# A linear-attention and quantised-ffn layer on one core: another order of the DMA queue, and another first turn

## The reference

```
xn  = LN(x)
q,k = elu(xn @ Wq.T + bq) + 1,  elu(xn @ Wk.T + bk) + 1      # 16 heads of 32 features
v   = xn @ Wv.T + bv
num = sum over d of q[t,d] * cumsum_t(k[t,d] * v[t,e])       # causal linear attention
den = max(sum over d of q[t,d] * cumsum_t(k[t,d]), 1e-6)
att = (num / den) @ Wo.T + bo
y   = x + LN(att)
yq  = y quantised in blocks of 32 features to the nearest value of an fp6 grid, times its block scale
wd  = the ffn weight, quantised in the same way
out = y + LN(yq @ wd.T + bias)
```

## Time and profile before

| | |
|---|---|
| median of the runs | 2397.83 us |
| the profiled execution | 2399.21 us, span 2397.4 us, mean granted clock 0.993 |
| TensorE matmuls | 2332.0 us busy, 97% |
| VectorE | 1984.1 us, 83% |
| GpSimd | 1470.3 us, 61% |
| ScalarE | 1080.8 us, 45% |
| DMA | 195.55 MB, 82 GB/s, 24.5% of 16 engines |

### The profile page before, as it was taken

One profiled execution on the slowest core, in us unless ns is written; L12 is line 12 of the kernel. 1 busy time (PEld: TensorE's weight loads), 2 busy tenths in 40 slices (PEclk: granted clock), 3 DMA queues, 4 the chain that ended last, 5 costly groups with the idle time before them and its releaser, 6 DMA issues.

```text
span 2397.4 us, 63827 instructions
## 1 busy us (share of the span) xinstructions
PE 2332.0 (97%) x26146; PEld 1905.0 (79%) x26146; DVE 1984.1 (83%) x3988; ACT 1080.8 (45%) x1840; POOL 1470.3 (61%) x1730
## 2 busy tenths in 40 slices
PE   7999999999999999999999999999999999999997
PEld 5877888888788788888787887888878888878785
DVE  7888889888788888898888887888988888878886
ACT  4444444444444444444444444444444444444442
POOL 2566566666566665666665665656666656656554
PEclk9999999999999999999999999999999999999999
DMA  4222221222222322222322222222123222223211
GB/s 158 71 92 98 75 77 62 88 99 73 86 65 75 99 90 80 77 65 86 99 73 90 73 71 91 96 76 75 62 89 99 73 90 73 71 91 95 77 46 37
DMA packets 108227, 195.55 MB, mean 82 GB/s; under 512 B 15136, under 2 KB 21664, under 8 KB 107424
## 3 DMA queue, kind: packets, MB, share of 16 engines
q1 hardware_dynamic: 107936, 191.47, 24.5%
HBM read 155.65 MB, written 35.78 MB: 80 GB/s over the span
## 4 chain that ended last, share of the span: by engine, by line
PE 79%; DMA 7%; DVE 4%; ACT 3%; issue 3%; POOL 2%; SPq 2%; POOLq 0%; DVEq 0%; ACTq 0%
PE work L423 12%; PE work L425 11%; PE work L424 11%; PE score L423 10%; PE score L424 10%; PE score L425 10%; PE work L540 5%; PE work L442 4%; PE score L505 4%; DMA rden_dram<-rinv 3%; DMA kc<-rden_dram 3%; PE state_bank L553 1%; POOL f_buf L1425 1%; DVE A L1020 1%; PE score L527 1%
## 5 line engine op out<-in xcount | busy, mean ns | idle before, releaser
L1020 DVE TENSOR_TENSOR A<-score,causal 128x512 f32<-128x512 f32 x512 | 329.2, 681 | 21.5 <-PE score L505 21.5
L1395 POOL TENSOR_TENSOR exp_t<-exp_t,x_coef 128x512 f32<-128x512 f32 x124 | 198.5, 1601 | 148.6 <-DMA exp_t<-in_xt 148.6
L725 ACT CAST oT_hi<-kc 128x512 fp32r<-128x512 f32 x128 | 79.6, 622 | 365.4 <-DVE kc L1015 365.4
L1402 POOL TENSOR_TENSOR x_res<-x_res,o_buf 128x512 f32<-128x512 f32 x128 | 175.6, 1372 | 104.5 <-ACT o_buf L670 104.5
L423 PE MATMUL work<-wo_hi,oT_hi 128*128 128x512 f32 x512 | 204.2, 399 | 14.8 <-ACT Kn L720 11.9
L423 PE MATMUL work<-wv_hi,xT_hi 128*128 128x512 f32 x512 | 214.9, 420 | 0.0
L423 PE MATMUL score<-xT_hi,wq_hi 128*128 128x512 f32 x512 | 208.1, 406 | 6.8 <-DVE KT L960 6.8
L1397 POOL TENSOR_TENSOR exp_t<-exp_t,x_coef 128x512 f32<-128x512 f32 x124 | 205.2, 1655 | 9.7
L423 PE MATMUL score<-xT_hi,wk_hi 128*128 128x512 f32 x512 | 205.7, 402 | 0.0
L425 PE MATMUL work<-wv_hi,xT_lo 128*128 128x512 f32 x512 | 202.2, 395 | 0.6 <-issue 0.6
L424 PE MATMUL work<-wv_lo,xT_hi 128*128 128x512 f32 x512 | 201.8, 394 | 0.9 <-issue 0.9
(11 more groups left out here) (134 smaller groups left out, 6393.1 us busy)
## 6 DMA issues: line engine op xcount, KB each, us to landing
x_in<-in_x SPq DMA_DIRECT2D x128, 256.0 KB, 4.3
x_res<-in_x SPq DMA_DIRECT2D x128, 256.0 KB, 2.8
kc<-rden_dram SPq DMA_DIRECT2D x128, 256.0 KB
exp_t<-in_xt SPq DMA_DIRECT2D x124, 256.0 KB, 3.1
out<-f_buf SPq DMA_DIRECT2D x96, 256.0 KB, 2.0
x_coef<-coef_dram SPq DMA_DIRECT2D x31, 512.0 KB, 3.8
out<-xd SPq DMA_DIRECT2D x32, 256.0 KB, 2.1
rden_dram<-rinv SPq DMA_DIRECT2D x32, 64.0 KB, 3.5
```

The costliest lines, as they stand in the source:

```text
L1020: nc.vector.tensor_tensor(A[:, j, :, :], score_bank[j][:], causal[:].unsqueeze(1).to_broadcast([P, G, P]), ALU.mult).then_inc(a_set, 1)
L1395: nc.gpsimd.tensor_tensor(rows, rows, by_token(0), ALU.mult).then_inc(x_scaled, 1)
L1402: nc.gpsimd.tensor_tensor(x_res[:, b, :], x_res[:, b, :], o_buf[:, b % 2, :], ALU.add).then_inc(r_set, 1)
```

## The change

- SyncE's order in a turn is rewritten. x by rows is loaded two tiles ahead (load_x(i + 2, b)), spread over the turn; the store and the spreads of the reciprocals go ahead of the loads of x by features, which are interleaved with the spreads; load_res(1), (2) and (3) go to the end of the turn, behind the last store and load_x(i + 2, 3).
- Wo is staged in x_res instead of kc, is loaded last of the weights, and is split behind the Q products; load_res of tile 0 waits for that. Wv comes before it.
- The last step of quantising the ffn weight, the product of the fp8 values with the scales, is made by GpSimd (dequantise_wf), no longer by VectorE.
- wf_transposes(0) and (1) run behind q(3), (2) and (3) behind v(0), through the banks work[2], work[1], work[2], work[0].
- The lists of ScalarE, VectorE and GpSimd are reordered to go with it, in the first turn and in the others.

```diff
-        W_DONE = {"k": G, "q": G + 1, "o": G + 2, "v": G + 3}
+        W_DONE = {"k": G, "q": G + 1, "v": G + 2, "o": G + 3}
-        wf_bank = [work[0], work[1]]
+        wf_bank = [work[2], work[1], work[2], work[0]]
...
             def load_res(tile, b):
                 if tile > 0:
                     sp.wait_ge(out_set, count(tile - 1, b))
+                else:
+                    sp.wait_ge(w_lo_set, W_DONE["o"])
...
             def turn(i, prev, cur, nxt):       # SyncE, as it is after
+                after = i + 2 < TILES
                 store(i - 1, 0)
                 load_x(i + 2, 0)
                 load_x(i + 2, 1)
                 store_coef(i + 1)
                 spread_coef(i + 1)
                 store(i - 1, 1)
                 load_x(i + 2, 2)
                 store_rden(i)
                 spread_rden(i, 0)
                 load_xt(i + 1, 0)
                 spread_rden(i, 1)
                 load_xt(i + 1, 1)
                 store(i - 1, 2)
                 spread_rden(i, 2)
                 load_res(i, 0)
                 load_xt(i + 1, 2)
                 spread_rden(i, 3)
                 load_xt(i + 1, 3)
                 store(i - 1, 3)
                 load_x(i + 2, 3)
                 load_res(i, 1)
                 load_res(i, 2)
                 load_res(i, 3)
...
+            for b in range(NSEQ):              # ahead of turn 0
+                load_x(1, b)
```

TensorE, first turn:

```diff
+                q(2)
+                q(3)
                 if first:
                     wf_transposes(0)
                     wf_transposes(1)
-                q(2)
-                q(3)
-                if first:
-                    wf_transposes(2)
-                    wf_transposes(3)
                 f(2)
                 xd_transposes(3)
                 past_products()
                 denominators()
                 v(0)
+                if first:
+                    wf_transposes(2)
+                    wf_transposes(3)
                 scores(0)
                 kn(0)
```

The end of the lists in the other turns, where the prediction looks:

```diff
 VectorE                                    # around normalise(0)
                 f_bias(3)
                 normalise(0)
-                o_lo(0)
-                f_seen(3)
                 mask(1, 0)
+                f_seen(3)
                 mask(1, 1)
+                o_lo(0)
+                x_lo(i + 1, 0)
                 v_bias(1)
...
                 greatest(i, 0)
                 scale(i, 0)
-                x_lo(i + 1, 3)
+                x_lo(i + 1, 2)
                 quantise(i, 0)
+                x_lo(i + 1, 3)
+                o_bias(i, 2)
                 normalise(3)
-                o_bias(i, 2)
-                r_seen(i, 1)
+                o_seen(i, 2)
                 o_lo(3)
+                r_seen(i, 1)
                 join(i, "r", 1)
                 widen(i, "r", 1)
 ScalarE
-                seed(0)
                 kn(0)
+                seed(0)
+                kn(1)
                 o_hi(0)
-                seed(1)
                 x_hi(i + 1, 0)
                 f_norm(2)
-                kn(1)
+                seed(1)
+                seed(2)
                 x_hi(i + 1, 1)
                 o_hi(1)
                 o_norm(i, 0)
 GpSimd
                 rstd(i - 1, "f", 1)
                 output(1)
+                rstd(i - 1, "f", 2)
                 x_scale(i + 1, 0)
-                rstd(i - 1, "f", 2)
+                output(2)
                 x_scale(i + 1, 1)
-                output(2)
                 rstd(i - 1, "f", 3)
```

More of the change, by code:

```diff
@@ L354, in turn @@
             def turn(i, prev, cur, nxt):
[L355 to L359, removed]
+                after = i + 2 < TILES
                 if prev:
                     store(i - 1, 0)
-                if cur:
-                    load_res(i, 0)
+                if after:
+                    load_x(i + 2, 0)
+                    load_x(i + 2, 1)
                 if nxt:
@@ L368, in turn @@
                     store(i - 1, 1)
[L369 to L373, removed]
+                if after:
+                    load_x(i + 2, 2)
                 if cur:
@@ L388, in turn @@
                     store(i - 1, 3)
+                if after:
+                    load_x(i + 2, 3)
                 if cur:
+                    load_res(i, 1)
+                    load_res(i, 2)
                     load_res(i, 3)
@@ L479, in v @@
                         take(pe, i, ("v", b), here, before)
+                        if first and b == 0:
+                            pe.wait_ge(wf_lo_set, 2)
                         weights(i, "v")
@@ L512, in kn @@
                         take(pe, i, ("kn", b), here, before)
+                        if first and b == 0:
+                            pe.wait_ge(wf_lo_set, G)
                         transposes(bank(("kn", b)), lambda g: KT[:, g, b, SEG - P:SEG]).then_inc(kn_tr, 1)
@@ L734, in seed @@
                     if cur:
+                        if first and b == 0:
+                            act.wait_ge(wf_lo_set, 3)
                         take(act, i, ("att", b), {0} if first else {-1, 0}, set())
@@ L767, in turn @@
                     k(2)
-                    carry(0)
-                    wf_high(0)
-                    wf_high(1)
                     k(3)
-                    carry(1)
                     q(0)
                     q(1)
+                    carry(0)
+                    q(2)
+                    carry(1)
                     carry(2)
-                    q(2)
+                    wf_high(0)
                     q(3)
+                    wf_high(1)
+                    high("o")
                     carry(3)
+                    for j in range(HPG):
+                        past(j)
                     wf_high(2)
                     wf_high(3)
-                    for j in range(HPG):
-                        past(j)
                     kn(0)
                     seed(0)
+                    o_hi(0)
                     seed(1)
-                    o_hi(0)
                     kn(1)
@@ L824, in turn @@
                 k(2)
+                o_norm(i - 1, 3)
                 carry(0)
-                o_norm(i - 1, 3)
+                k(3)
+                carry(1)
+                r_norm(i - 1, 2)
                 xd_hi(1)
-                r_norm(i - 1, 2)
-                carry(1)
                 r_norm(i - 1, 3)
-                k(3)
-                q(0)
-                carry(2)
-                f_norm(0)
+                f_norm(0)
+                carry(2)
+                q(0)
                 xd_hi(2)
@@ L856, in turn @@
                 kn(2)
-                seed(2)
+                o_hi(2)
+                seed(3)
+                kn(3)
                 f_norm(3)
@@ L1236, in turn @@
                 join(i - 1, "o", 3)
-                scan(0)
+                r_seen(i - 1, 2)
                 widen(i - 1, "o", 3)
                 phi_k(1)
-                r_seen(i - 1, 2)
+                scan(0)
+                phi_k(2)
                 scan(1)
                 f_bias(0)
-                phi_k(2)
-                if nxt:
-                    widen(i + 1, "x", 1)
                 join(i - 1, "r", 2)
+                f_seen(0)
                 widen(i - 1, "r", 2)
                 r_seen(i - 1, 3)
-                if nxt:
-                    x_seen(i + 1, 3)
@@ L1277, in turn @@
                     widen(i + 1, "x", 3)
+                phi_q(0)
+                phi_q(1)
+                xd_lo(2)
+                phi_q(2)
+                product(2)
+                phi_q(3)
+                f_seen(1)
                 join(i - 1, "f", 1)
-                phi_q(3)
-                product(2)
                 widen(i - 1, "f", 1)
                 product(3)
-                f_bias(2)
                 xd_lo(3)
-                f_seen(2)
                 clamp()
                 invert()
-                join(i - 1, "f", 2)
+                f_bias(2)
@@ L1478, in turn @@
                 dequantise(i - 1, 2)
+                output(0)
                 if nxt:
                     rstd(i + 1, "x", 2)
-                output(0)
+                product(0)
                 dequantise(i - 1, 3)
-                product(0)
                 product(1)
```

202 lines of the change are left out of this document (102 added, 100 removed).

## The result

The changed kernel takes 2459.43 us, median of 4 runs (2457.53 to 2465.69), against 2397.15 for the kernel before in the same comparison: ratio 1.0266, 95% interval 1.0244 to 1.0289. It is 62 us slower, where 12 were forecast. Slower was right, the size was not, and 2459 lies outside the range of 2378 to 2431.

What follows compares the result with a forecast made beforehand. TensorE, busy 97% of the span, was taken as the bound, so only its gaps count. Terms -17 + 34.5 - 6 + 0.5 = +12 us on the median 2397.83 gave 2410 us, range 2378 to 2431.

Steps and rivals of the forecast that it cites:

- Part 1: Reciprocals' store ahead of both x-by-feature loads: spread(0) 2 us earlier, waits at o(0) and for A gone, -17 us.
- Part 2: x-by-feature loads behind the reciprocals: load_xt(0) lands about 3.5 us later, residual(0) and output(3) 0.3 us late.
- rival D: x-by-feature load 1 us later still, chain 1.2 us late, attend(1) waits for x_lo(0): 2.0 us per turn, 2435, chance 0.15.
- Part 3: load_res(1) at the queue's end: residual(1) 1.9 us late, TensorE waits 1.15 us per turn at xd transposes, +34.5 us.
- no cover: Behind the xd transposes on TensorE: k(1) and everything else stand there, with no idle time to absorb the wait.
- my 4.4: End-of-turn burst: the third queued 256 KB transfer lands 4.4 us after the first issue, as the profile rows show.
- Part 4: First turn with weights reordered: q(0) starts at 28.45 after 3.1 us idle, attend(1) at 66.1, -6 us.
- "Issue" waits: TensorE waits in the denominators, released by no engine, 9.9 us in 8: to stay, bounds -5 and +10 us.
- The tail: Last turn: the same late load_res(1), one place earlier in the burst, +0.5 us.

Runs made afterwards that it cites:

- e10: e7's queue and first turn, but with the changed kernel's lists of ScalarE, VectorE and GpSimd: 2376.2 us, 0.9915 of the kernel before.
- e7: e6 with load_xt(1) also moved, to between the reciprocals' store and the first spread: 2368.0 us, 0.9876 of the kernel before.
- e12: Changed kernel with load_x(i + 2, 2) moved from ahead of the reciprocals' store to behind load_xt(3): 2428.6 us, 1.0130 of the kernel before.
- e3: Changed kernel with load_xt(0) and load_xt(1) again ahead of the reciprocals' store from turn 1 on: 2420.2 us, 1.0108 of the kernel before.
- e2: Changed kernel with load_res(1) right behind store(1) and load_res(2) behind store(2), from turn 1 on: 2467.4 us, 1.0309 of the kernel before.
- e6: Kernel before with the new first turn and load_res(1) moved from ahead of the x-by-feature loads to behind the four spreads: 2372.3 us, ratio 0.9894.
- e11: e7 with load_res(1) moved to the end of the turn, behind store(3): 2405.9 us, 1.0032 of the kernel before.
- e1: Kernel before with only the changed kernel's first turn; steady lists and queue stay old: 2389.5 us, ratio 0.9978.
- e9: e7 with x by rows loaded two tiles ahead, none of it ahead of the reciprocals: 2371.2 us, 0.9894 of the kernel before.
- e5: Changed kernel's first turn and DMA queue, with the kernel before's ScalarE, VectorE and GpSimd lists from turn 1 on: 2555.3 us, 1.0650 of the kernel before.
- e4: Changed kernel with the edits of both e2 and e3: 2443.3 us, 1.0200 of the kernel before.
- e8: Changed kernel with the kernel before's DMA queue from turn 1 on, so the new lists alone: 2406.8 us, 1.0044 of the kernel before.

## Why the prediction was wrong

**Part 1, reciprocals first: the first step that failed.** It held that the store "goes out about 1 us earlier", that "with 512 KB fewer ahead of its 64 KB it lands about 1 us quicker", that spread(0) goes out 2 us earlier, and that o(0) stops waiting: -17 us. By the medians the store goes out 0.6 us sooner after rinv (0.4 for 1.0) and lands 0.4 us quicker (3.0 for 3.5). From rinv to the first spread it is 4.0 us for 5.0, so 1 us was gained and not 2. The 512 KB is right as a count of the queue: load_res(1) and the two loads of x by feature leave the place in front of the store, load_x(i + 2, 2) comes there. What it left out is that the 512 KB of coefficients come 2.7 us later (1.4 of it by the new lists alone, e10 against e7), so that they are unfinished when the store is issued; the prediction had them "still issued about 2 us before the denominators", and it is 0.7 us (2.2 before). e12 takes the load of x by rows away: 3.1 us, which is the forecast gain of 2 us, and 31 us of the time. The rest went because rinv itself comes 1.3 us later in its turn, behind the new waits at o(3) and at the xd transposes; the first spread leaves 0.3 us later than before the change. At o(0) TensorE still waits 8.2 us, where it was 11.7, and the short waits for A (3.7 us) are gone; on the view's numbers this saved 7 us, not 17.

**Part 2, x by feature: the second step, and the costliest.** It had the landing 3.5 us later; it was 6.3 (x_scale(0) at 49.1 against 42.8). Of the difference 2.3 us is part 1's spread(0), which leaves 0.3 us later and not 2 us sooner; the rest of 0.5 is open. It had residual(0) 0.3 us late with a bound of 1.2; it was 2.8. And it put nothing for the two places where TensorE waits for that chain. o_hi(1) stands behind x_hi(1), and with it o(1) behind x_scale(1): 28 waits, 18.6 us. attend(1) stands behind x_lo(0): 12 waits, 18.8 us, which only rival D named. e3 shows it: with those loads put back, both kinds of wait are gone, and 39 us of the time. Rival D was nearly this case; its price of 2435 at 15% was too low, in part because it kept all of part 1's saving.

**Part 3, the late residual load: the lateness right, its effect not.** residual(1) starts 4.1 us after store(3) is issued, by the median, and 2.5 us before the change: 1.6 later, where 1.9 was forecast. The xd wait is 16 us and not 34.5, and taking it away saves nothing (e2). That TensorE is by then late itself, at o(3) and through the x chain, is my reading of why it is half; no run isolates it. The sentence that there is no cover was wrong. The price worked out from the Trainium skill (page "DMA: Bandwidth & Descriptors", section "Anatomy of one DMA"), an estimate of 3.8 us for the third transfer in a burst, was a little nearer than my 4.4: in the turn shown it took 4.0, from the output store at 1061.03 to residual(1) at 1065.00. The page gives that price for a transfer that GpSimd issues, and here SyncE issues them. The rule of the Trainium skill to issue a transfer early (same page, section "Rules for kernel authors") does not tell where the residual load should stand in these queues: issued earlier it lost 8 us (e2), issued later it gained 17 (e6), and at the very end it lost 38 (e11 against e7).

**Part 4, the first turn: right in sum, by luck in part.** -6 us forecast, -6.3 in the trace, -5 in the time of e1. The way differed. q(0) waited 1.39 us and not 3.1, at full clock where the prediction kept the low one, and attend(1) came at 63.37, not 66.1, which is 8.5 us sooner than before. About 2 of these were lost again before turn 1 began.

**"Issue" waits** in the denominators went from 9.9 to 4.3 us, with -5 to +10 as bounds. **The tail** +1.0 for +0.5.

The sum by parts, forecast and measured: part 1, 2 and 3 together +17.5 and +63.7; first turn -6 and -6.3; tail +0.5 and +1.0. Measured in spans that is +58.3, and 62 in the medians of the runs. By waits of TensorE the steady turns' +63.7 are +37.4 at o(1) and attend(1), +16.2 at the xd transposes, +9.4 at o(3), -7 on the way of the reciprocals, some 5 less of "issue" waits, and +13 of busy time. Why VectorE and ScalarE are late for o(3) in 20 turns was not isolated.

## What to carry to other kernels

Where one queue carries both prefetches and a round trip that an engine waits for, count the bytes that are still unfinished ahead of the round trip at the moment it is issued: those that a change puts there as well as those it takes away, and those that come there because another engine's list moved. Moving one 256 KB prefetch from there to a later place was worth 0.6 us in every turn in e6 and 1.0 us in e12; moving one more into the time in which the queue's issuer waits for the round trip brought 0.1 us (e7), within the noise. Distance by itself ("two tiles ahead") was worth nothing (e9). And a load that is issued behind the round trip inherits all its delays: ask which engine's list has that load's work ahead of work that the busy engine waits for. A list of orders is made for one queue: judge queue and lists apart and together, because here they cost 166, 17 and 70 us.

## What was not expected of the hardware

A 64 KB store took from 2.5 to 4.2 us to land (medians), longer by and large with the bytes of other transfers that were unfinished when it was issued. With 461 KB by the mean it took 2.5 to 2.6 us (e5, e7, e9, e11), with 725 KB 2.5 (e12) and 2.8 (e6), with 922 KB 3.0 (after) and 3.5 (e10), with 964 KB 3.5 (before, e1), with 990 KB 3.9 (e2), with 1186 to 1237 KB 4.1 (e3) and 4.2 (e4, e8). Why equal counts differ by up to 0.5 us stays open. The traces also tell what the late spread of the coefficients, 512 KB, has to do with it. In the changed kernel the store took 3.2 us in the 25 turns in which that spread was unfinished and 2.6 in the other 5; in e10 it was 3.6 in 24 turns and 3.0 in 6.

TensorE's granted clock fell in the steady turns of the kernel before three times, each time after an "issue" wait of over 2 us. TensorE's timeline at one of them, and the stretch behind it:

```profile
642.63 0.65 PE L493 MATMUL work<-kc,den_sel 128*32 128x128 f32 x8 [2.69 <-issue]
```

```profile
642.57:645.98 3.41, 3.35 (x15) 2.39 (x16) 1.29 (x3) 0.00 (x0) 0.67 (x1) 0.50 0.77 244
```

In the changed kernel's steady turns, with a longest wait of 1.9 us, it never fell. A wait of that length did not always spare the clock, nor a longer one always lower it: in e4 it fell after one of 1.8 us and held after one of 2.1.

What the "issue" waits are no run isolates. In the kernel before each of the 12 that stand in the steady turns ended 2.2 to 2.8 us after the start of a 16 KB packet of an instruction queue, of which the trace has 206 in 2397 us (the page's line is below). So TensorE may have waited there for its own instructions. Why these waits are shorter in the changed kernel was not tried.

```profile
q8 instruction: 206, 3.38, 0.6%
```
